# First mixture: the gates reach all partitions through device memory instead of through TensorE and ScalarE

## The reference

```python
probs_full = softmax(x @ router_w.T)             # 64 experts
probs, idx = top_k(probs_full, 2)
order = argsort(idx.reshape(-1), stable=True)    # choices sorted by expert
keep = pos < CAP                                 # an expert keeps its first 128 choices
h = gelu(buf @ w1.T + b1); y = h @ w2.T + b2     # the same weights for every expert
gate = where(keep, flat_p, 0)
out[tok] += y[slot] * gate
```

## Time and profile before

| | |
|---|---|
| three runs | 1668.86, 1669.5, 1673.58 us (median 1669.5) |
| the profiled execution | 1673.58 us, of which the span is 1671.8 us |
| busy over the span | PE 95%, PEld 70%, DVE 74%, ACT 55%, POOL 47% |
| the first mixture | first products at 842.0 us, last gated half at 972.65 us |
| instructions of the gates' way, all 13 groups | PE 65 turns, ACT 26 copies, DVE 13 copies |

### The profile page before, as it was taken

One profiled execution on the slowest core, in us unless ns is written; L12 is line 12 of the kernel. 1 busy time (PEld: TensorE's weight loads), 2 busy tenths in 40 slices (PEclk: granted clock), 3 DMA queues, 4 the chain that ended last, 5 costly groups with the idle time before them and its releaser, 6 DMA issues. The chain is left out here.

```text
span 1671.8 us, 62551 instructions
## 1 busy us (share of the span) xinstructions
PE 1589.5 (95%) x24380; PEld 1169.5 (70%) x24380; DVE 1242.6 (74%) x3629; ACT 912.6 (55%) x2409; POOL 784.4 (47%) x932
## 2 busy tenths in 40 slices
PE   7999999899999999997999998999999999879997
PEld 3333334677777777776567746888888888669997
DVE  2799926888888888885767764577777777778875
ACT  0111315666666666663544455666666666557753
POOL 0000000788888888885011102345555555645554
PEclk9999999999999999999989999999999999979998
DMA  9999940000000000000300000000000000135431
GB/s 338 355 373 355 350 160 1 3 4 4 3 4 4 4 4 4 3 4 10 106 1 1 1 1 6 3 9 21 25 18 25 18 25 18 37 114 152 137 85 41
DMA packets 73078, 118.06 MB, mean 71 GB/s; under 512 B 11627, under 2 KB 30366, under 8 KB 72828
## 3 DMA queue, kind: packets, MB, share of 16 engines
q1 hardware_dynamic: 65054, 100.04, 18.2%
q0 software_dynamic: 6096, 12.94, 2.2%
q10 hardware_dynamic: 1678, 1.43, 0.3%
HBM read 97.59 MB, written 18.61 MB: 70 GB/s over the span
## 5 line engine op out<-in xcount | busy, mean ns | idle before, releaser
L1700 PE MATMUL ps<-xn,s_a_wqkv 128*128 128x260 f32 x1024 | 277.4, 403 | 6.1 <-DMA s_a_wqkv<-in_f_b 3.0
L1700 PEld LDWEIGHTS ps<-xn,s_a_wqkv 128*128 128x128 f32 x1024 | 178.0, 192 | 52.0 <-issue 18.4
L1037 POOL TENSOR_TENSOR prob_a<-e_a,inv_sum_a 128x512 f32<-128x512 f32 x64 | 67.1, 1048 | 194.8 <-issue 113.4
L1566 DVE TENSOR_REDUCE neg_max_a<-ps 128x8 f32<-128x520 f32 x128 | 89.2, 697 | 73.3 <-PE ps L1674 50.2
L2323 POOL DMA_INDIRECT out<-h,xn x93 | 97.8, 1051 | 88.3 <-DVE h L2438 86.8
L1784 PE MATMUL ps<-s_a_wqkv,xn_pair_a 128*64 128x256 f32 x1024 | 138.9, 391 | 0.0
L1092 ACT ACTIVATE resT_a<-ps 128x260 f32<-128x260 f32 x256 | 85.2, 386 | 97.2 <-PE ps L1751 61.0
L1021 POOL TENSOR_TENSOR kept_a<-e_a,keep_a 128x585 f32<-128x585 f32 x64 | 87.2, 1362 | 70.4 <-issue 60.3
L921 POOL MEMSET cls_queries_a<- 128x1040 f32 x2 | 1.9, 966 | 250.9 <-POOLq L430 250.9
L1751 PE MATMUL ps<-probT_a,horner_a 64*64 64x65 f32 x2048 | 113.2, 228 | 2.0 <-DVE horner_a L1312 1.5
L1741 PE MATMUL ps<-dv_a,probT_a 64*64 64x64 f32 x2048 | 107.1, 223 | 3.0 <-DVE probT_a L1325 2.3
(11 more groups left out here) (305 smaller groups left out, 4663.6 us busy)
## 6 DMA issues: line engine op xcount, KB each, us to landing
x_chunk<-in_x_main SPq DMA_DIRECT2D x144, 512.0 KB, 11.0
xn<-pair_rows SPq DMA_DIRECT2D x93, 130.0 KB, 2.1
pair_rows<-pad_rows_m SPq DMA_DIRECT2D x29, 130.0 KB
s_f_all<-in_f_w SPq DMA_DIRECT2D x2, 1024.0 KB
x_ends<-in_x_tail SPq DMA_DIRECT2D x16, 96.0 KB, 5.6
out<-h,xn POOLq DMA_INDIRECT x93
s_w_tok<-in_w_tok SPq DMA_DIRECT2D x6, 192.0 KB, 8.9
pair_rows<-rows_m,slot_i_m POOLq DMA_INDIRECT x65, 2.5
```

The source lines that it names most:

```text
L1566: last = nc.vector.tensor_reduce(neg_max[:, :, 0:CH], score(), AX.X, ALU.min)
L1700: nc.tensor.matmul(ps[:, QK_BANK[i], 0:QUAD], w_qkv[:, c * P:(c + 1) * P], xn[:, t.h * QUAD:(t.h + 1) * QUAD], start=True, stop=True).then ...
```

## The change

The gates no longer go through TensorE and ScalarE. `spread_gate`, `copy_gate`, `gate_wide` and their semaphores are gone. There is a new tensor in device memory, `gate_rows`, one row of 640 numbers for each group, and SyncE gets a program for this stage. For each group it waits for the gates, stores them in token order (partition p's five numbers go to places p, 128 + p, ...), waits until the store has landed, and loads the row back onto all 128 partitions. `gated` waits for that load, and the write of `gate_r` waits for the store of two groups before.

```diff
-        gate_w = sb("gate_wide", [P, 2, T, P])
...
-            def spread_gate(g):
-                pe.wait_ge(wide_done, g + 1)
-                since(pe, bc_done, 2 * g)
-                for k, (t0, t1) in enumerate(PARTS):
-                    for t in range(t0, t1):
-                        last = nc.tensor.transpose(ps[:, 2 + k, (t - t0) * P:(t - t0 + 1) * P],
-                                                   gate_w[:, g % 2, t, :], ident[:, :])
-                    last.then_inc(bc_ps, 1)
...
-                        if i % 2 == 1 and c == 2:
-                            spread_gate(g)
...
-            def copy_gate(g):
-                since(act, y_done, 2 * g - 2)
-                for k, (t0, t1) in enumerate(PARTS):
-                    act.wait_ge(bc_ps, 2 * g + k + 1)
-                    nc.scalar.activation(gate_all[:, g % 2, t0 * P:t1 * P], ps[:, 2 + k, 0:(t1 - t0) * P],
-                                         ACT.Copy).then_inc(bc_done, 1)
...
+                since(dve, row_out, 16 * (g - 1))
                 nc.vector.tensor_tensor(gate[:, sl], gsum[:, sl], inv[:, sl], ALU.mult).then_inc(gate_done, 1)
-                dve.wait_ge(gate_done, g + 1)
-                since(dve, bc_ps, 2 * g - 2)
-                nc.vector.tensor_copy(gate_w[:, sl], gate[:, sl].unsqueeze(2).to_broadcast([P, T, P]))\
-                    .then_inc(wide_done, 1)
...
-                dve.wait_ge(bc_done, 2 * g + 2)
+                dve.wait_ge(gate_in[g % 2], 16 * (g // 2 + 1))
...
+        @block.sync
+        def _(sp):
+            for g in range(G):
+                sp.wait_ge(gate_done, g + 1)
+                sp.dma_start(gate_rows[g, :].rearrange("(t p) -> p t", p=P), gate[:, g % 2, :],
+                             allow_slow_non_contiguous=True).then_inc(row_out, 16)
+                sp.wait_ge(row_out, 16 * (g + 1))
+                since(sp, y_done, 2 * g - 2)
+                sp.dma_start(gate_all[:, g % 2, :], gate_rows[g:g + 1, :].to_broadcast([P, GN]))\
+                    .then_inc(gate_in[g % 2], 16)
```

More of the change, by code:

```diff
@@ L2002, in attention, with routed_mlp @@
         stage_block.close()
-def routed_mlp(nc, tokens, h, xn, ps, routed, expert_ids, before, all_ones, ident, w1, b1, w2, b2):
+def routed_mlp(nc, tokens, h, xn, ps, routed, gate_rows, expert_ids, before, all_ones, w1, b1, w2, b2):
     T = routed.T
@@ L2044, in routed_mlp @@
         sum_done, total_done = sem("gate_sum_r_s"), sem("total_done_r")
-        inv_done, gate_done, wide_done = sem("inv_done_r"), sem("gate_done_r"), sem("wide_done_r")
-        bc_ps, bc_done = sem("gate_ps_r"), sem("gate_all_done_r")
+        inv_done, gate_done = sem("inv_done_r"), sem("gate_done_r")
+        row_out, gate_in = sem("gate_row_out_r"), [sem(f"gate_all_in_r{k}") for k in range(2)]
         up_ps, g_done = sem("up_ps"), sem("gelu_done")
@@ L2049, in routed_mlp @@
         block = ctx.enter_context(nc.Block())
-        PARTS = ((0, 3), (3, T))
         def since(eng, sm, value):
@@ L2122, in gelu @@
                                      bias=b1[:, c:c + 1]).then_inc(g_done, 1)
-            def copy_gate(g):
-                since(act, y_done, 2 * g - 2)
-                for k, (t0, t1) in enumerate(PARTS):
-                    act.wait_ge(bc_ps, 2 * g + k + 1)
-                    nc.scalar.activation(gate_all[:, g % 2, t0 * P:t1 * P], ps[:, 2 + k, 0:(t1 - t0) * P],
-                                         ACT.Copy).then_inc(bc_done, 1)
[L2131 to L2135, removed]
+            for i in range(2 * G):
+                for c in range(C):
+                    gelu(i, c)
         @block.vector
@@ L2535, in vit_tower @@
             layer_norm(nc, "f0", tokens, h, xn, ps, center_w, mean_w, spread_w, rest, stale=stale, router=routed)
-            routed_mlp(nc, tokens, h, xn, ps, routed, S["expert_ids"], S["before"], S["all_ones"], S["ident"],
+            gate_rows = nc.dram_tensor("gate_rows", (groups, T * P), FP32, kind="Internal").ap()
+            routed_mlp(nc, tokens, h, xn, ps, routed, gate_rows, S["expert_ids"], S["before"], S["all_ones"],
                        S["f0_w1"], S["f0_b1"], S["f0_w2"], S["f0_b2"])
```

## The result

The changed kernel takes 1766.23 us (median of 4 runs, 1763.97 to 1767.56) against 1670.66 before (4 runs): ratio 1.0569, 95% interval 1.0548 to 1.059. It is 95.6 us slower, where 6.5 us faster was forecast, and far outside the range. The side is the first rival's; the size is ten times what that rival gave.

The account below looks back on a forecast made before the run. TensorE was taken to bound the stage. Removing turns saved 7.2 us, but the end, 111.65 + L with L 5.4, gave 117.05 against 123.5: 1669.5 - 6.5 = 1663.0 us, range 1661 to 1664.5, all cases 1661 to 1679.

Parts of the forecast that it names:

- the first rival: Gates' store is late: each 4-byte piece takes a DMA engine 58 ns, load slow; +9.4 us, 1678.9; chance 0.22.
- What bounds the stage: In the first mixture, TensorE sets the pace, with no gap in 10 us; a group lasts 9.82 us.
- the turns' 7.2 us: TensorE's turns of the gates cost 0.555 us a group on the path; removing 13 saves 7.2 us.
- the stretch: Time from the first gates to the last gated half; 123.5 us before, forecast 117.05.
- The round and its formula: Per group, `gated` to next gates takes 3.34 us, then L; the whole is 40.6 + 13 L, 110.8 at 5.4.
- L: Time from the gates' end to the start of `gated(2g)`: store, load and hand-offs; 5.4 us, ends 4.1 and 7.1.
- The point L = 6.38: The value of L at which the change in the kernel's time is zero.
- The store: Writing a group's gates to device memory, 640 pieces of 4 bytes: 2.4 us to landing, ends 1.7 and 3.6.
- The load: Bringing one row of gates to 128 partitions, 320 KB: 2.7 us, ends 2.1 and 3.2.
- A round that is just exposed: Second rival, in the gates' round: L about 6.2, 121.2 us for the stretch, -2.3 us, 1667.2; chance 0.16.
- turns that free nothing: Third rival, on TensorE: its freed 0.555 us goes into another wait, time stays 1669.5; chance 0.04.

Follow-up runs that it names:

- partition order: Changed kernel with each partition's five gates stored side by side, 128 pieces of 20 bytes, tokens' gates mixed up; 1669.95 us, before 1668.68.
- the full result in partition order: Changed kernel storing 128 pieces of 20 bytes, with `gated` reading the row with a stride in two instructions per half; 1665.91 us, ratio 0.9971.
- one tile: Changed kernel storing only the first of five tiles, 128 pieces of 4 bytes, loading an input row instead; 1738.03 us, before 1668.68.
- lines side by side: Changed kernel storing 16 partitions only, 80 pieces of 4 bytes within 320 bytes, loading an input row instead; 1712.14 us, before 1669.11.
- 8 bytes apart, partition order: Changed kernel storing 640 pieces of 4 bytes, 8 bytes apart, each partition's together, loading an input row instead; 1690.51 us, before 1669.71.
- 8 bytes apart, token order: Changed kernel storing 640 pieces of 4 bytes, 8 bytes apart, neighbours from neighbouring partitions, loading an input row instead; 1691.6 us, before 1669.71.
- one tile, 8 bytes apart: Changed kernel storing only one tile, 128 pieces of 4 bytes, 8 bytes apart in place of 4; 1678.15 us.

## Why the prediction was wrong

- *What bounds the stage, and the turns' 7.2 us.* Right for the stage: with a quick store (partition order) the stretch shrinks by 6.8 us where 6.5 was forecast. By total time less was seen, 1.9 us without any transfer over 10 runs, an interval that reaches no change, and 4.8 with the full result in partition order over 12. Where the rest goes is open.
- *The round and its formula.* Right: 218.7 worked out, 218.9 measured, with L put in as measured (the two medians alone; the steps between, 0.3 us in the prediction, come to 0.12 in the round shown). It holds for the other slow stores as well. With L as the mean store and mean load of each trace, 40.6 + 13 L gives the stretch within 0.6 us every time:

  | store | L, us | 40.6 + 13 L | measured |
  |---|---|---|---|
  | as changed | 13.68 | 218.4 | 218.9 |
  | one tile | 11.31 | 187.6 | 188.1 |
  | lines side by side | 9.37 | 162.4 | 162.9 |
  | 8 bytes apart, partition order | 7.82 | 142.3 | 142.7 |
  | 8 bytes apart, token order | 7.44 | 137.3 | 137.9 |
  | one tile, 8 bytes apart | 6.64 | 126.9 | 127.4 |

  The point L = 6.38 fits too: these are all over it and longer than 123.5, the partition-order store with L of 5.3 is under it and shorter.
- *The store.* The step that failed: "The 32 more cost between nothing and 32 x 58 ns = 1.9 us. A piece has 4 bytes against 1,040, so I take about 10 ns each, 0.3 us, and 2.1 + 0.3 = 2.4 us." The engines' part was right (7.5 ns a piece), and with the pieces 64 bytes apart the store did take 2.2 us. What was put at nothing is what follows behind the engines: the pieces meet again in device memory, 128 of them in each 512 bytes, and the store took 10.0 us where 2.4 was forecast. That is 7.6 us a group, 13 times. Both ends, 1.7 and 3.6, were drawn from the engines' side only, from rows whose pieces were whole rows of 1,040 bytes.
- *The load.* Too low by 1.0 us (3.7 against 2.7), over its upper end of 3.2. Alone this would have put L at 6.4 and the gain at zero.
- *The first rival* had the right side and the right place, the store, and the rule of the Trainium skill that it quoted ("DMA: Bandwidth & Descriptors", Rules for kernel authors: one descriptor per element) holds: 640 pieces for 640 numbers, by the count of packets. Whether small pieces are read, modified and written, as the other rule it quoted has it, no run shows. The rival's price was wrong for the same reason: it looked for the cost at the engines. Small pieces alone are not slow here, since 80 of 4 bytes landed in 1.4 us, close together on lines far apart.
- *The other rivals.* A round that is just exposed did not occur, and turns that free nothing did not either, by the stretches of 116 to 118 us with a quick store or none.

## What to carry to other kernels

Before a small result goes through device memory, lay it out so that each partition writes one piece, and let the reader do the turning: 128 pieces of 20 bytes landed in 1.4 us, the same bytes in 640 interleaved pieces in 10.0, and in 640 pieces 64 bytes apart in 2.2. Where a chain of waits closes on itself once a group, write down its length against the pace of the bounding engine: here 3.3 us plus the transfers against 9.3, and every us over it is paid once a group, 13 times. For a transfer of a shape that no row shows, an upper end from the nearest row is no upper end.

## What the runs showed of the hardware

- Small writes to device memory that lie close together hold each other up after the DMA engines are done: 80 pieces of 4 bytes land in 6.1 us when their five lines of 64 bytes touch, in 1.4 when the lines are 1 KB apart.
- A load with a store of such pieces close behind it can land late: 8.9 us in place of 3.7, with its bytes moved 3.5 us before. It did so in 11 of 21 cases; that the store is the cause is not shown.
- A load of 320 KB takes 3.2 us whether each partition reads a row of its own or all 128 read one row.
- After a stop TensorE goes on at the lower of its two levels: in the kernel that weighs a group earlier it had waited 5.40 us before 899.71, as its row says; the granted clock is 1.00 until 898, 0.69 from 898 to 899, 0.50 from 899 to 905 and 1.00 from 906 on.
